# Local attention of a megakernel: softmax weights divided on Pool, the heads' output copied by DVE, the output product moved ahead of the transposes

## What is computed

```
for l in range(2):
    q, k, v = split(shift_token(x) @ wqkv[l])          # 8 heads of 64
    q, k = l2norm(q) * qs, l2norm(k) * ks, rotary on both
    sim  = q @ k.T        # each window of 64 sees itself and the 64 tokens before, masked
    attn = softmax(sim)   # maximum, exponential, sum, division
    o    = attn @ v
    x    = x + o @ wo[l]
    ... feed-forward part on shift_token(x), then the next l
```

## Time and profile before

| | us |
|---|---|
| median of 3 runs | 2592.55 (2589.67 to 2597.14) |
| the profiled execution | 2598.66 |
| its span in the trace | 2596.8 |
| PE busy in the span | 2143.8 (83%) |
| DVE busy | 1920.6 (74%) |
| ACT busy | 1427.7 (55%) |
| POOL busy | 595.1 (23%) |

### The profile page before, as it was taken

How to read it: one execution, slowest core, us unless ns; L and a number is a source line. 1 busy time by engine, 2 the same in 40 slices (tenths; PEclk the granted TensorE clock), 3 DMA queues, 4 the chain that set the end, 5 groups by cost and what they waited for, 6 DMA issues and landing times.

```text
span 2596.8 us, 46373 instructions
## 1 busy us (share of the span) xinstructions
PE 2143.8 (83%) x17328; PEld 1198.6 (46%) x17328; DVE 1920.6 (74%) x4139; ACT 1427.7 (55%) x2642; POOL 595.1 (23%) x416
## 2 busy tenths in 40 slices
PE   5996899787799589878779958987788995988877
PEld 4673123556467222354647722236464761223645
DVE  7657896777765789678675579967777457996677
ACT  4342677747334267674733427867463342776755
POOL 3621001331253100124034210021505330004040
PEclk9997799898899689989889969998998995999989
DMA  4002100110000300001000030010100002001010
GB/s 147 1 1 74 27 10 11 28 23 15 17 1 1 84 16 10 18 21 31 15 9 1 1 86 18 8 28 11 31 13 9 1 23 64 19 10 31 5 31 21
DMA packets 58894, 63.16 MB, mean 24 GB/s; under 512 B 17264, under 2 KB 44208, under 8 KB 58160
## 3 DMA queue, kind: packets, MB, share of 16 engines
q1 hardware_dynamic: 55480, 57.26, 8.7%
q10 hardware_dynamic: 3192, 2.90, 0.4%
HBM read 24.68 MB, written 15.01 MB: 15 GB/s over the span
## 4 chain that ended last, share of the span: by engine, by line
PE 49%; DVE 28%; ACT 14%; issue 6%; DMA 2%; SPq 1%; POOL 0%; ACTq 0%; DVEq 0%; POOLq 0%
PE PS L1390 45%; DVE arena L1145 10%; ACT arena L760 7%; DVE arena L1244 2%; ACT arena L703 2%; PE PS L1718 1%; DVE s_at L1219 1%; DVE arena L1212 1%; DMA tmp<-xf 1%; DVE tmp L1219 1%; ACT tmp L714 1%; DVE arena L1331 1%; PE PS L1408 1%; ACT x_in L774 1%; DVE xn L899 1%
## 5 line engine op out<-in xcount | busy, mean ns | idle before, releaser
L1390 PE MATMUL PS<-arena 128*32 128x256 f32 (+5 forms) x10304 | 826.8, 350 | 149.2 <-DVE arena L1145 50.9
L1145 DVE TENSOR_REDUCE arena<-PS 128x1 f32<-128x512 f32 x1024 | 641.4, 687 | 50.2 <-PE PS L1390 50.2
L1390 PEld LDWEIGHTS PS<-arena 128*32 128x32 f32 (+5 forms) x10304 | 322.0, 122 | 648.6 <-DVE arena L1145 270.5
L703 ACT ACTIVATE arena<-PS 128x1024 f32<-128x1024 f32 x512 | 516.7, 1026 | 180.3 <-PE PS L1390 179.0
L655 ACT ACTIVATE arena<-PS 128x512 f32<-128x512 f32 x256 | 150.8, 598 | 245.5 <-PE PS L1390 245.4
L1390 PEld LDWEIGHTS PS<-w2e,arena 128*128 128x128 f32 x2048 | 246.0, 192 | 49.7 <-issue 49.7
L1108 DVE TENSOR_TENSOR arena<-PS,arena 128x512 f32<-128x512 f32 x128 | 86.5, 689 | 217.5 <-PE PS L1390 217.1
L1390 PE MATMUL PS<-w2e,arena 128*128 128x128 f32 x2048 | 247.4, 275 | 0.0
L760 ACT ACTIVATE arena<-PS,arena 128x128 f32<-128x128 f32 x512 | 231.3, 552 | 23.1 <-DVE arena L1281 22.0
L1390 PE MATMUL PS<-wqkv,arena 128*128 128x512 f32 x384 | 181.1, 612 | 25.5 <-ACT arena L742 21.7
L505 POOL TENSOR_TENSOR zz<-zz,arena 128x512 f32<-128x512 f32 x104 | 135.3, 1301 | 274.1 <-DVE arena L1108 245.7
(11 more groups left out here) (304 smaller groups left out, 3272.3 us busy)
## 6 DMA issues: line engine op xcount, KB each, us to landing
arena<-arena SPq DMA_DIRECT2D x120, 128.0 KB, 2.3
scr_q<-arena SPq DMA_DIRECT2D x40, 128.0 KB, 2.4
scr_k<-arena SPq DMA_DIRECT2D x40, 128.0 KB, 2.5
arena<-scr_k SPq DMA_DIRECT2D x24, 200.0 KB
arena<-scr_q SPq DMA_DIRECT2D x24, 192.0 KB
x_in<-in_x SPq DMA_DIRECT2D x5, 512.0 KB, 4.8
out_x<-tmp SPq DMA_DIRECT2D x4, 512.0 KB, 3.8
wqkv<-in_wqkv SPq DMA_DIRECT2D x1, 1536.0 KB, 9.2
```

What stands on the lines that cost most here:

```text
L703: act.activation(pb[:, n % 8], pair(2 * (n % 2)), ACT.Exp).then_inc(S["p"], 1)
L1145: dve.tensor_reduce(mxp[:, h % 2, j, t, hf:hf + 1], PS[:, ring_bank("mx", h, n), :], AX, ALU.max)\
L1390: return pe.matmul(o, w, v, start=start, stop=stop, **kw)
```

## The change

- POOL takes over product(t): a loop of 8 multiplications a pass, each waiting for the new semaphore `rlr`, which recip(t) on DVE raises. recip(t) waits for product(t-3) (`pn`).
- olT(t) moves from ACT, turn t+3, to DVE, turn t+4, where it stands behind bias(u) and ahead of add(u-6).
- On PE, ol(u-4) moves ahead of tr(u-2) in the same turn.

```diff
+                    for u in range(T):
+                        m = l * T + u
+                        pool.wait_ge(S["rlr"], m + 1)
+                        v = pl[:, m % 3]
+                        pool.tensor_tensor(v, v, bc(rl[:, m % 3], [P, 2, 4, KEYS], 3), ALU.mult).then_inc(S["pn"], 1)
...
-                        if 3 <= u <= T + 2:
-                            q = n - 3
-                            act.wait_ge(S["o_lps"], q + 1)
-                            if q >= 2:
-                                act.wait_ge(S["ol_ps"], q - 1)
-                            act.copy(olT[:, q % 2], PS[:, 6, :].rearrange("p (c n) -> p c n", c=4))\
-                                .then_inc(S["olT"], 1)
...
-            with nc.Fori(0, B, engines=(dve.engine,), hint_back_edge=True) as b:
+            with nc.Fori(0, B, engines=(dve.engine,), hint_back_edge=True, head_slot={dve.engine: 0}) as b:
...
                             dve.wait_ge(S["p_exp"], 8 * (m + 1))
-                            link(dve.reciprocal(rl[:, m % 3], sl[:, m % 3]))
-                            v = pl[:, m % 3]
-                            dve.tensor_tensor(v, v, bc(rl[:, m % 3], [P, 2, 4, KEYS], 3), ALU.mult).then_inc(S["pn"], 1)
+                            if m >= 3:
+                                dve.wait_ge(S["pn"], m - 2)
+                            dve.reciprocal(rl[:, m % 3], sl[:, m % 3]).then_inc(S["rlr"], 1)
...
+                        if 4 <= u <= T + 3:
+                            q = n - 4
+                            dve.wait_ge(S["o_lps"], q + 1)
+                            if q >= 2:
+                                dve.wait_ge(S["ol_ps"], q - 1)
+                            dve.tensor_copy(olT[:, q % 2], PS[:, 6, :].rearrange("p (c n) -> p c n", c=4))\
+                                .then_inc(S["olT"], 1)
                         if u >= 6:
                             t = u - 6
                             dve.wait_ge(S["ol_ps"], l * T + t + 1)
...
+                        if 4 <= u <= T + 3:
+                            t = u - 4
+                            q = l * T + t
+                            pe.wait_ge(S["olT"], q + 1)
+                            pe.wait_ge(S["xf"], 2 * T * l + t)
+                            for c in range(4):
+                                ins = mm(PS[:, 7, 0:W], olT[:, q % 2, c], res["wol"][:, l, c],
+                                         start=(c == 0), stop=(c == 3))
+                            ins.then_inc(S["ol_ps"], 1)
                         if 2 <= u <= T + 1:
                             m = n - 2
                             pe.wait_ge(S["pn"], m + 1)
...
-                        if 4 <= u <= T + 3:
-                            t = u - 4
```

More of the change, by code:

```diff
@@ L243, in build @@
         st_ps p pv on on_moved ot_ps tn ob_ps otn xab op_ps op_rd x2 s1
-        sh_ps hsh0 hsh1 hcp_v hT_ps hT hT_late qkv_ps sq rotb rqe qkr kq_ps kq vl s_lps ml p_exp pn ssq ssq_ok rq0 rot vz ptd pt_ps pt o_lps olT ol_ps xf
+        sh_ps hsh0 hsh1 hcp_v hT_ps hT hT_late qkv_ps sq rotb rqe qkr kq_ps kq vl s_lps ml p_exp rlr pn ssq ssq_ok rq0 rot vz ptd pt_ps pt o_lps olT ol_ps xf
         ffn_tile g_ps a_ps gl hg y2_ps xb gfin obuf
@@ L349, in _ @@
             sp.sem_inc(S["out_gone"], 1)
-            with nc.Fori(0, B, engines=(sp.engine,), hint_back_edge=True) as b:
+            with nc.Fori(0, B, engines=(sp.engine,), hint_back_edge=True, head_slot={sp.engine: 0}) as b:
                 x_next = d["x"][bass.ds(b + 1, 1)].rearrange("a (t p) w -> p (a t) w", p=P)
@@ L481, in _ @@
             pool.tensor_scalar(gam[:], res["ln_gamma"][:], sc[:, 10:11], None, ALU.mult).then_inc(S0["casts"], 1)
-            with nc.Fori(0, B, engines=(pool.engine,), hint_back_edge=True) as b:
+            with nc.Fori(0, B, engines=(pool.engine,), hint_back_edge=True, head_slot={pool.engine: 0}) as b:
                 for c in range(CH):
@@ L574, in _ @@
             act.wait_ge(S0["act0"], 3)
-            with nc.Fori(0, B, engines=(act.engine,), hint_back_edge=True) as b:
+            with nc.Fori(0, B, engines=(act.engine,), hint_back_edge=True, head_slot={act.engine: 0}) as b:
                 link = stepper(act, S["act_step"])
@@ L748, in _ @@
                             act.activation(sc[0:1, 9:10], ident[0:1, 0:1], ACT.Exp)
-                    for u in range(T + 4):
+                    for u in range(T + 2):
                         n = T * l + u
@@ L1409, in transposes @@
                         .then_inc(S[done], 1)
-            with nc.Fori(0, B, engines=(pe.engine,), hint_back_edge=True) as b:
+            with nc.Fori(0, B, engines=(pe.engine,), hint_back_edge=True, head_slot={pe.engine: 0}) as b:
                 pe.wait_ge(xn_tiles, b * T + T)
```

## The result

The changed kernel takes 2679.18 us (median of 4 runs, 2676.62 to 2683.74), the kernel before 2594.67 beside it (2589.67 to 2597.14): 1.0333 times as long, 95% interval 1.0315 to 1.0352, or about 85 us more. Times of passes and stretches come from one profiled execution of each kernel.

What follows compares the result with a forecast made beforehand. ACT bounds the middle of a pass, PE close behind, latency its end. From scores(6) to add(7) +9.6 us, less 0.2, is +9.4 a pass; eight passes +75, so 2668 us against the 2592.55 median; range 2635 to 2700.

Steps and rivals of the forecast that it cites:

- The large term: PE and DVE order: ol ahead of tr waits for an add behind max, bias and olT; turn 5.59 us, not 4.49.
- the stretch from scores(6) to add(7): Last part of a pass on PE and DVE: 34.4 us in all, before 24.78.
- the turn: PE's turns 5 and 6, from scores to scores: 6.3 us with bias held, where it was 4.49.
- the way from scores(7) to o(4): PE entering the end phase: 7.4 us, before 5.47, as o(4) now waits for tr and an uncovered copy5.
- The end step: From one o to the next in the end phase: one serial chain of 5.23 us; three take 15.7, before 10.87.
- the end, o(7) to add(7): Last chain of a pass, through olT, adds and ol: 5.0 us, before 3.95.
- the hold: bias on DVE waits until POOL's product ends: 0.7 us a turn; no or smaller hold, 2656 us, had 12%.
- The clock: Rival: PE partly at 1.2 GHz in the end phase, some 6 us more a pass, 2715 us; chance 10%.
- a clock well below 1.00 in the end phase: Sign on PE that would show the prediction wrong; no size given.
- The loop heads: Placing of the loops' heads: taken as 0 us, with bounds of 11 either way.
- The product on POOL: Product moved off DVE: 2.1 us long, late by about 1 us, nobody waits for it; by itself worth nothing.
- olT's leaving ACT: ACT's turn falls to 4.0 us; worth 0.2 a pass and nothing else, nothing in the end phase.

Runs made afterwards that it cites:

- order_back: The changed kernel with ol(u-4) on PE behind tr(u-2) again, all else as changed: 2585.17 us, 0.9977 of before.
- add_first: The changed kernel with add(u-6) moved to the head of DVE's turn, ahead of recip, max, bias and olT: 2584.56 us, 0.9968 of before.
- filler runs: Two versions of the changed kernel with four idle PE products ahead of ol: at ol(4) to ol(7) 2660.62 us, at ol(0) to ol(6) 2655.41 us.
- heads_only: The kernel before with the five loop heads placed and nothing else: 2581.59 us, 0.9949 of before.
- pool_only: The kernel before with the product moved to POOL and nothing else: 2596.15 us, 1.0007 of before.
- mixed4: The kernel before with product on POOL, loop heads placed, and olT on DVE for a pass's first four tiles, then on ACT: 2557.18 us, 0.9866 of before.
- order_only: The kernel before with only ol moved ahead of tr on PE; olT stays on ACT, product on DVE: 2621.69 us, 1.0105 of before.
- dve_product: The changed kernel with the product back on DVE, behind recip: 2674.19 us, 1.0312 of before.
- filler_all: The changed kernel with four idle products on PE ahead of each of ol(0) to ol(6): 2655.41 us, 1.0245 of before.

## Why the prediction was right, and what it had wrong

- **The large term.** That ol ahead of tr waits for an add behind max, bias and olT was right, and its size was near. Shown by order_back and add_first, which each take away one half of the mechanism, and with it 77 and 69 us in the passes (94 and 95 in all), the falls of the clock there among them. That the stretch from scores(6) to add(7) came out at 34.58 us for the 34.4 forecast is in part luck: 1.35 of it is the step at the lower clock. Without that it is 33.2; the turn was forecast 0.5 too long and the way from scores(7) to o(4) 0.6 too long (7.4, measured 6.82).
- **The end step** of 5.23 measured 5.15, for the chain forecast; the end, o(7) to add(7), 5.12 for 5.0.
- **The turn** was 5.84, not 6.3. The term that was mis-sized is the hold: bias is held 0.18 us, not 0.7. Three things went into it. POOL's product takes 1.90 instead of 2.1. It starts at scores(6) + 1.05 instead of + 1.21, so that it ends at + 2.95 where + 3.31 was forecast. And the held bias ends with POOL's product, 0.02 behind it, while the forecast let it start there and run its 0.17 behind; that the record of L1228 showed the former was read but not used. Of the 0.7 these take 0.20, 0.16 and 0.15. The turn without a hold was sized right: 5.59 forecast, 5.84 less 0.18 is 5.66.
- **The clock** was given 10% as a rival with +47 us. It fell, but for less: it made one step 6.50 instead of 5.15 here, and in other passes single steps from one add to the next are 0.5 to 1.5 us longer than the rest. With every step at its shortest, passes would be about 55.2 long, so the falls are an estimated 2.1 of the 10.41 a pass: 17 us, and the passes would cost +66 without them, where +75 was forecast. The filler runs gave back 10 and 8 us in the passes, 19 and 24 in all. The prediction named a clock well below 1.00 in the end phase as a sign that it is wrong; in single stretches that sign came.
- **The loop heads**, taken as 0 with bounds of 11 either way, are -13. In the changed kernel the three stretches over the edges are only 7 us shorter, 2.3 each, though ACT's stop there is gone as well (3.63 us idle ahead of its first instruction). In heads_only they are 17 shorter, but its profiled execution is its fastest (2577.34, median 2581.59), that of before lies 4 to 6 above the medians (2598.66), and its clock over the edges is higher. The changed kernel's stretches behind a pass that ends at a clock of 0.50 are 5 us longer (478.8, 478.9) than the one behind a pass that ends at 1.00 (473.9); before, the stretches differ by the same 5 us with every pass ending at 1.00, so the end of the pass alone isn't the reason.
- So the total was as good as it was by errors that cancel: +75 and 0 were forecast; by the profiled executions, which lie 80 us apart, it is +66 for the chain, +17 for the clock in passes (both by the estimate above), -7 at the edges and +3 elsewhere. The lesson of the numbers is that the sum of the chain was sound, that the hold was too large and the clock too small.
- **The product on POOL and olT's leaving ACT** were costed at nothing. For the product, pool_only shows it (1.0007). For the copy, "the 0.2 and nothing else" was too little: mixed4 shows that it is worth most where a pass goes over into its end phase, where before has waits of 1.18 and 1.43 us for olT. The first stood in the earlier trace rows and was not costed. The 0.2 itself came: the turn ahead of scores(6) fell from 4.50 to 4.26. In the changed kernel none of this shows, which fits the longer chain over the add there.
- Of the views forecast, the releaser (L1293) came as said, and so did two of the three end steps (5.15 for 5.2, the third 6.50). The waits are 1.55 in the turns, within the 1.4 to 2.1 said, but 1.07 in the end phase. bias had 0.36 at most where 0.8 to 0.9 was expected, and L544 takes 1.90 for 2.1. ACT's gap ahead of copy4, 1.73 us, was as said.

**What stays open.** Outside the passes the kernels differ by up to 29 us, of which the placed heads explain some 7 and the edits nothing more. The profiled executions spend there 2219.5 us before, 2216.0 in the changed kernel, 2205.8 in order_only, 2197.4 in heads_only, 2196.9 in order_back and 2190.7 in add_first. So 19 of the 94 us of order_back and 25 of the 95 of add_first are not the wait of ol. Their passes begin up to 5 us apart (first max from 484.2 to 489.6). The granted clock goes with the time: its mean outside the passes is 0.903 in the changed kernel, 0.916 in heads_only and in order_back, and 0.923 in add_first, and over all eleven kernels with placed heads a longer time outside goes, nearly without exception, with a lower clock there. That the clock is the whole reason is argued; what sets it in these stretches, no run tells.

## What to carry to other kernels

Moving an instruction ahead on an in-order engine moves its wait with it: before ol goes ahead of tr, ask when its operand's buffer comes free, and count everything that stands ahead of the releasing instruction in the other engine's queue. If the wait can't be avoided, move the releaser instead (one addition at the head of its turn was worth 95 us here, 69 of them in the passes). A placement that helps while an engine is saturated can lengthen the chain when the pipeline drains, so choose it per phase: four tiles one way and four the other gave the best version.

## What was not expected of the hardware

- A product on POOL with one value repeated along the row takes 1.90 us for 1024 elements, and twice the 1.04 of 512 elements would be 2.08.
- Of two instructions of POOL that stand 0.07 us apart, only the first held DVE: bias ended 0.01 behind it and 0.06 ahead of the second.
- A copy of 64 elements within SBUF on DVE (L1263 of mixed4), 0.19 us otherwise, took 1.32 and 1.83 beside POOL's product, and ended 0.05 behind it both times. DVE had to wait for PE behind it both times, so it delayed nothing there.
- The granted clock of PE fell to 0.76 and 0.67 in windows with PE busy 1.93 and 2.07 of 3 us, and gaps of about 1 us; in the window just ahead (527 to 530), also with 2.07 busy, it was 1.00, and end steps with the same gaps ran at 1.00 throughout in seven passes of dve_product. Four products that nobody reads, 1.1 us in each gap, kept it at 1.00 in every end phase of filler_all; the two kernels with such products were 19 and 24 us faster than the changed one.
- Placing the heads of five loops at the start of a fetch block took a stop of 3.8 us from ACT at an edge, and 13 us of 2594 from the kernel, of which some 7 are the stop's.
